# A weight part on a second DMA queue, an image block in two halves, and a later place for the small vectors, at the start of a vision-transformer block

## The reference

```python
# x: 32 images of 3 x 96 x 96; patches of 16 x 16; D = 256, 37 tokens per image (one class token, 36 patches)
patches = patchify(x)                                   # (32, 36, 768)
tokens  = einsum('bnd,ed->bne', patches, W) + b
h       = concatenate([cls_token, tokens], 1) + pos_embedding
paths   = sigmoid(h @ Wp + bp)                          # 8 heads, depth 5
agree   = pq * pk + (1 - pq) * (1 - pk)
sim     = cumprod(agree, -1).sum(-1) / 5                # causal mask, softmax
h       = layernorm(h + softmax(sim) @ (h @ Wv) @ Wo)
y       = silu(layernorm_affine(h) @ w1 + fc1_bias)     # w1, w2 dequantised from int32
h       = layernorm(h + 0.5 * (y @ w2 + fc2_bias))
```

## Time and profile before

| | |
|---|---|
| times of three runs | 176.03, 178.40, 178.91 us |
| profiled execution | 176.34 us |
| span in the trace | 174.6 us |
| PE busy | 154.1 us, 88% of the span |
| DVE, ACT, POOL busy | 94.3, 48.0, 55.6 us |
| first matmul | 6.09 us after the span's start |

### The profile page before, as it was taken

How to read it: one execution, slowest core, us unless ns; L and a number is a source line. 1 busy time by engine, 2 the same in 40 slices (tenths; PEclk the granted TensorE clock), 3 DMA queues, 4 the chain that set the end, 5 groups by cost and what they waited for, 6 DMA issues and landing times.

```text
span 174.6 us, 2987 instructions
## 1 busy us (share of the span) xinstructions
PE 154.1 (88%) x1141; PEld 122.0 (70%) x1141; DVE 94.3 (54%) x175; ACT 48.0 (27%) x105; POOL 55.6 (32%) x129
## 2 busy tenths in 40 slices
PE   0289999799989999899999999999879969979980
PEld 0177878577667797487887778887658858868760
DVE  0065047557777956728647587647547443634232
ACT  0412112523243335114235324226022311032100
POOL 5009811032082603427107218106334022530011
PEclk9999999999999999999999999999999999999999
DMA  5999999700000000000100010000010000000000
GB/s 141 241 241 248 232 369 375 280 2 4 0 2 6 2 0 4 0 0 8 34 0 0 0 34 0 30 4 0 0 32 4 30 0 0 30 34 0 0 30 30
DMA packets 5501, 10.67 MB, mean 61 GB/s; under 512 B 715, under 2 KB 4400, under 8 KB 5232
## 3 DMA queue, kind: packets, MB, share of 16 engines
q1 hardware_dynamic: 5248, 10.30, 20.1%
q10 hardware_dynamic: 240, 0.19, 0.5%
HBM read 9.27 MB, written 1.21 MB: 60 GB/s over the span
## 4 chain that ended last, share of the span: by engine, by line
PE 83%; DVE 6%; DMA 4%; ACT 2%; POOL 2%; issue 1%; ACTq 1%; POOLq 0%
PE bank_z L555 20%; PE bank_s L542 18%; PE bank_z L436 7%; DMA vec_rows<-in_L_ffn_ln_beta 4%; PE bank_s L412 4%; PE bank_p L451 4%; PE bank_s L479 3%; PE bank_p L452 3%; PE bank_s L537 2%; PE bank_w L493 2%; PE bank_p L427 2%; PE bank_o L508 2%; PE bank_o L509 2%; PE bank_z L427 2%; PE bank_o L517 2%; PE bank_w L497 2%
## 5 line engine op out<-in xcount | busy, mean ns | idle before, releaser
L555 PE MATMUL bank_z<-w,act 128*128 128x256 f32 (+1 forms) x160 | 37.0, 381 | 1.8 <-DVE res L830 1.8
L542 PE MATMUL bank_s<-hnT,w 128*128 128x256 f32 (+1 forms) x160 | 35.2, 362 | 0.0
L555 PEld LDWEIGHTS bank_z<-w,act 128*128 128x128 f32 (+1 forms) x160 | 28.1, 182 | 8.0 <-issue 3.2
L542 PEld LDWEIGHTS bank_s<-hnT,w 128*128 128x128 f32 x160 | 28.9, 190 | 5.0
L821 DVE SCALAR_TENSOR_TENSOR act<-th,bank_s 128x512 f32<-128x512 f32 (+1 forms) x20 | 13.0, 648 | 20.3 <-ACT th L691 20.1
L337 POOL TENSOR_TENSOR rstd<-var,exponents 128x3 f32<-128x3 f32 (+1 forms) x10 | 8.9, 893 | 46.9 <-DVE var L805 46.9
L691 ACT ACTIVATE th<-bank_s 128x512 f32<-128x512 f32 (+1 forms) x20 | 11.3, 565 | 32.4 <-PE bank_s L542 32.4
L792 DVE RECIPROCAL recip<-bank_w 128x222 f32<-128x222 f32 (+1 forms) x11 | 16.4, 1494 | 0.7 <-PE bank_w L497 0.7
L675 ACT ACTIVATE phi_q<-bank_p 128x222 f32<-128x222 f32 (+1 forms) x11 | 3.9, 351 | 32.6 <-PE bank_p L461 32.6
L436 PE MATMUL bank_z<-xT,wT 128*128 128x288 f32 x48 | 12.6, 413 | 0.0
L787 DVE TENSOR_TENSOR probs<-probs,allowed 111x888 f32<-111x888 f32 (+1 forms) x11 | 11.5, 1046 | 1.9 <-ACT probs L685 1.9
(11 more groups left out here) (107 smaller groups left out, 242.0 us busy)
## 6 DMA issues: line engine op xcount, KB each, us to landing
x_rows<-in_x SPq DMA_DIRECT2D x6, 576.0 KB, 13.7
q<-in_L_ffn_fc_q SPq DMA_DIRECT2D x2, 1024.0 KB, 20.1
s<-in_L_ffn_fc_scales SPq DMA_DIRECT2D x2, 1024.0 KB, 22.1
out<-fin SPq DMA_DIRECT2D x9, 128.0 KB, 1.7
w_rows<-in_L_tok_W SPq DMA_DIRECT2D x3, 256.0 KB, 8.2
wvp<-in_L_attn_Wv SPq DMA_DIRECT2D x1, 256.0 KB, 10.2
wo<-in_L_attn_Wo SPq DMA_DIRECT2D x1, 256.0 KB, 17.1
b<-in_L_ffn_fc_bias ACTq DMA_DIRECT2D x1, 128.0 KB, 9.6
```

The source lines that it names most:

```text
L542: last = mm(block[:, i], w1[:, e, f * 128:(f + 1) * 128], hnT[p % 2][:, e, 0:n], start=False, stop=(i == 1 and e == E2 - 1))
L555: last = mm(bank_z[0:w, 0:D], act2[:, f, in_pair(b)], w2[:, f, :], start=(f == 0), stop=(f == FB - 1))
```

## The change

Four things change.

The first weight part moves from SP's queue to ACT's, as the first issue there, ahead of `pos_rows` and the vectors. Its size stays.

The first image block is issued first on SP, as two transfers of 8 of the 16 image rows each, with a semaphore for each (`x0_in`). DVE sorts each half as it comes (`by_half_patch`), so `x_pat_ready` counts one more from there on. `turn_block` waits for each half apart.

`turn_vectors` moves on PE from ahead of `turn_block(0)` to between `project_channel(0, 0)` and `project_channel(0, 1)`, and its result from `bank_w` to an unused end of bank 1 of `bank_s` (`vec_bank`). Because of that `turn_block(1)` waits for the last step of `position_columns`.

The order on PE up to the third block is another, and `project_channel` of channel 0 goes by k first and e second.

```diff
@@ SP
-            for c in range(C):
+            top = x[0:HALF, 0].rearrange("b (g o i) w -> b g o (i w)", o=2, i=PATCH // 2)
+            for ih in range(2):
+                sp.dma_start(x_rows[:, 0, ih * HALF_PATCH:(ih + 1) * HALF_PATCH], top[:, :, ih]).then_inc(x0_in[ih], 16)
+            for c in range(1, C):
                 sp.dma_start(w_rows[:, :, c * 256:(c + 1) * 256], w_by_channel[c]).then_inc(w_in[c], 16)
                 x_block(c)
@@ ACT
+            act.dma_start(w_rows[:, :, 0:256], w_by_channel[0]).then_inc(w_in[0], 16)
             act.dma_start(pos_rows[:], pos.rearrange("o t d -> (o t) d")).then_inc(pos_in, 16)
@@ PE
             def turn_block(n):
-                pe.wait_ge(x_pat_ready, n + 1)
                 for ih in range(2):
+                    pe.wait_ge(x_pat_ready, n + 2 if n > 0 else ih + 1)
+                    if n == 1 and ih == 0:
+                        pe.wait_ge(posb_step, 1 + E2)
...
+                order = [(e, k) for e in range(E2) for k in (2 * n, 2 * n + 1)]
+                if n == 0:
+                    order = [(e, k) for k in (0, 1) for e in range(E2)]
...
             turn_weight(0)
-            turn_vectors()
             turn_block(0)
             project_channel(0, 0)
+            turn_vectors()
+            project_channel(0, 1)
             turn_weight(1)
             turn_block(1)
-            pe.wait_ge(posb_step, E2)
-            pe.wait_ge(vec_ready, 1)
-            project_channel(0, 1)
+            project_channel(1, 0)
             turn_weight(2)
-            project_channel(1, 0)
+            project_channel(1, 1)
             turn_block(2)
-            project_channel(1, 1)
             project_channel(2, 0)
@@ DVE
+            def by_half_patch(ih):
+                dve.wait_ge(x0_in[ih], 16)
+                dve.tensor_copy(x_pat[:, 0, :, ih * 128:(ih + 1) * 128].rearrange("p g (i j) -> p g i j", i=PATCH // 2),
+                                x_rows[:, 0, ih * HALF_PATCH:(ih + 1) * HALF_PATCH].rearrange(
+                                    "p (i g j) -> p g i j", i=PATCH // 2, g=GRID)).then_inc(x_pat_ready, 1)
...
-            by_patch(0)
+            by_half_patch(0)
+            by_half_patch(1)
             x_columns(0)
             position_columns()
```

More of the change, by code:

```diff
@@ L46, in vit_block @@
     PARTS = 3
+    HALF_PATCH = PATCH * IMG // 2
     FIRST = NTOK % 128
@@ L108, in vit_block @@
         bank_z = ps("bank_z", [128, 512])
+        vec_bank = bank_s[:, 1, 3 * HR:512]
         ident = sb("ident", [128, 128])
@@ L181, in vit_block @@
         w_in = [sem(f"w_in{i}") for i in range(C)]
+        x0_in = [sem(f"x0_in{i}") for i in range(2)]
         x_in = [sem(f"x_in{i}") for i in range(2 * C)]
@@ L396, in turn_vectors @@
                 pe.wait_ge(weight_set, 5)
+                pe.wait_ge(xT_dve, 1)
                 for e in range(E2):
-                    pe.transpose(bank_w[:, e * T:(e + 1) * T], pos_rows[:, e * 128:(e + 1) * 128], ident[0:T, 0:T])
+                    pe.transpose(vec_bank[:, e * T:(e + 1) * T], pos_rows[:, e * 128:(e + 1) * 128], ident[0:T, 0:T])
                 at = E2 * T
-                pe.transpose(bank_w[:, at:at + N_VEC], vec_rows[:], ident[0:N_VEC, 0:N_VEC])
-                pe.transpose(bank_w[:, at + N_VEC:at + N_VEC + 1], weight_row[:].rearrange("o i a b -> o (i a b)"),
+                pe.transpose(vec_bank[:, at:at + N_VEC], vec_rows[:], ident[0:N_VEC, 0:N_VEC])
+                pe.transpose(vec_bank[:, at + N_VEC:at + N_VEC + 1], weight_row[:].rearrange("o i a b -> o (i a b)"),
                              ident[0:1, 0:1]).then_inc(vec_psum, 1)
             def turn_block(n):
-                pe.wait_ge(x_pat_ready, n + 1)
                 for ih in range(2):
+                    pe.wait_ge(x_pat_ready, n + 2 if n > 0 else ih + 1)
+                    if n == 1 and ih == 0:
+                        pe.wait_ge(posb_step, 1 + E2)
                     if n > 0:
@@ L422, in project_channel @@
                 pe.wait_ge(wT_ready, n + 1)
-                for e in range(E2):
-                    for k in (2 * n, 2 * n + 1):
-                        if c == 0 and e == 0:
-                            pe.wait_ge(xT_act if k % 2 else xT_dve, n + 1)
-                        last = mm(first_half_bank(c, e)[:, 0:CP], wT[:, k, e * 128:(e + 1) * 128], patches(k, c),
-                                  start=(k == 0), stop=(k == KT - 1))
-                    if n == C - 1:
+                order = [(e, k) for e in range(E2) for k in (2 * n, 2 * n + 1)]
+                if n == 0:
+                    order = [(e, k) for k in (0, 1) for e in range(E2)]
+                for e, k in order:
+                    if c == 0 and (k, e) in ((2 * n, 0), (2 * n + 1, 0)):
+                        pe.wait_ge(xT_act if k % 2 else xT_dve, n + 1)
+                    last = mm(first_half_bank(c, e)[:, 0:CP], wT[:, k, e * 128:(e + 1) * 128], patches(k, c),
+                              start=(k == 0), stop=(k == KT - 1))
+                    if k == KT - 1:
                         last.then_inc(tok_psum, 1)
@@ L748, in position_columns @@
                 at = E2 * T
[L749 to L750 removed]
+                dve.tensor_copy(vec_cols[:], vec_bank[:, at:at + N_VEC]).then_inc(posb_step, 1)
+                dve.tensor_copy(weight_col[:], vec_bank[:, at + N_VEC:at + N_VEC + 1]).then_inc(vec_ready, 1)
                 dve.wait_ge(posb_step, 1)
                 for e in range(E2):
[L753 to L754 removed]
+                    ts(posb[:, e, 1:T], vec_bank[:, e * T + 1:(e + 1) * T], tokb_col[:, e:e + 1], None, ALU.add)
+                    tt(posb[:, e, 0:1], vec_bank[:, e * T:e * T + 1], cls_col[:, e:e + 1], ALU.add).then_inc(posb_step, 1)
             def class_tokens():
```

4 lines of the change are left out of this document (removed).

## The result

Twenty executions of the changed kernel had a median of 177.82 us, twenty of the kernel before on the same chips 177.0 us. Every ratio in this document leaves out executions over 1.5% above the fastest of their kernel; the two medians alone would give 1.0046. The ratio is 1.0083 with a 95% interval of 1.0055 to 1.0111: slower by some 1.5 us, where no change was forecast. The base of the forecast, 177.4 us, lay 0.4 us above the median measured for the kernel before, so 177.82 came within 0.4 us of the forecast time although the change itself was missed: that is luck.

The account below looks back on a forecast made before the run. PE bounds the kernel, block 0 its start, with the vectors level. Vectors at 14.0 plus 12.28 us put the third block at 26.28 against 26.25: no change, 177.4 us, between bases 176.4 and 178.4; range 174.2 to 180.8.

Parts of the forecast that it names:

- Landing of block 0's second half (6.5): First loads on SP's queue: second half lands at 6.5 us, no earlier than 6.0 and no later than 8.9.
- The fourth case: Block 0 still lands at 8.4 to 8.9, bound by engines, not queue; 0.0 to +0.5 us; chance 0.12.
- Landing of the vectors (14.0): ACT's queue: vectors land at 14.0 us, bounds 9.6 to 16.6, stalling PE about 2 us from 11.8.
- the second case: Vectors come at 11.8 or before: -2.15 us, 174.2 on the profiled execution, 176.2 on the median; chance 0.18.
- the third case: Vectors land with block 2 at 16.6, PE idle from 11.8: 2.6 to 5.0 us slower, 179.0 to 181.3; chance 0.18.
- Weight part (6.0): First weight part, issued at 0.79 on ACT's queue, lands 5.2 us later, at 6.0.
- Full rate (10.9): PE, working without a break from 6.0, reaches its full rate 4.9 us later, at 10.9.
- The eight rows: Channel 0's four products on block 0, eight matmul rows on PE, run from 9.2 to 11.8, partly at half rate.
- Lost covers (0.4): Projections of channels 1 and 2: second product waits for ACT's copy, 0.2 us each.
- Third block (26.28): PE starts the third block at 14.0 + 12.28 = 26.28 us against 26.25 before: no change.
- Biases on POOL: POOL's first bias step moves from 13.1 to about 18 us, at no cost.

Follow-up runs that it names:

- the split: Changed kernel with the 37 position rows loaded as 32 and 5 rows; ratio 1.0020 to the kernel before.
- loads alone: Kernel before with only the new loads, vectors still turned ahead of block 0; ratio 1.0055 to the kernel before.
- the rows twice: Changed kernel loading the same 37 position rows a second time into a tile nobody reads; ratio 1.0311 to the kernel before.
- before, split: Kernel before with the 37 position rows loaded as 32 and 5 rows; ratio 1.0008 to the kernel before.
- The middle order: Changed kernel with each block again turned ahead of a projection covering its copies, DVE sorting block 1 before its position steps; ratio 1.0020 to the kernel before.

## Why the prediction was wrong

**Landing of block 0's second half (6.5): failed, and it decided when PE came to the vectors.** Measured 9.02, outside the bounds of 6.0 to 8.9 that were given. The value was argued from the queue: nothing stood ahead of it there. But the position rows use one engine, and that engine's six packets of the half start only behind the 37 rows (6.45 to 7.71, the other 90 by 5.74); without the rows beside it the half was early, with the split (6.34) and with the rows issued last (6.45). The prediction knew the one engine and used it against the vectors only. The fourth case (0.12) had the landing nearly right (8.4 to 8.9, and `x_pat` at 9.4, which came at 9.60), though it put it to all engines. The rule of the Trainium skill that was weighed against the change (DMA: Bandwidth & Descriptors, section Issuing engines are not separate DMA queues) is borne out in the time: with the rows split the weight part's queue made no difference (0.9885 and 0.9881). The 9.02 against 8.86 is no test of it, since the rows kept back both.

**Landing of the vectors (14.0): failed.** With these loads they were there at 10.2 (loads alone), and there was no stall; the second case had that (0.18). The sum let the rows wait until the weight part was through at 6.0. It was through at 4.0: issued ahead of the rows it was not kept back by them, and it went side by side with SP's loads (69.5% of the engines). That rows on one engine can come very late was right as a mechanism: PE got them at 17.2 with the rows twice and at 17.1 with the rows last, and 1.031 and 1.047 in the time, which is the third case's stall from another cause.

**Weight part (6.0): mis-sized,** 4.07. The 5.2 us were carried over from before, where the rows kept the part back (with the rows split it came at 3.98 there). The 2 us gave PE nothing, since the next thing was the half.

**Full rate (10.9): failed.** The sum took the 4.9 us from first work to full rate in the trace of before as a rule. It came at 13.4 after, and from 1.8 us after the first product (before, split) to 8.6 us (after, split). The eight rows took 3.22 us and not 2.6. Extra transposes in the idle time left it where it was in two kernels, and in one brought it to 7.1 for a while; what sets the moment stays open.

**Lost covers (0.4): mis-sized,** 1.2, and this is what made the third block late. The chain of the kernel before has, for comparison:

```profile
18.97 0.44 PE bank_s L389 x4
19.41 0.97 PE bank_p L427 x4
20.38 0.97 PE bank_o L427 x4
21.35 0.99 PE bank_s L412 x12
```

Channel 1's first projection takes 2.47 us (18.58 to 21.05) against 0.97 + 0.97 = 1.94 there, 0.5 more; from the turning of block 2 to the third block it is 3.61 us (23.43 to 27.04) against 0.99 + 1.94 = 2.93, 0.7 more. The prediction counted ACT's copy less one product, 0.2 each time. But ahead of channel 2 PE waits 0.45 us for DVE's copy, which had no cover at all and was not in the sum, and the product behind each wait takes longer too (0.75 instead of 0.48, and 1.21 for two instead of 0.97). With the second projection of channel 0 done and block 1 turned, the changed kernel was 0.4 us ahead (18.58 against 18.97 for the same work); 1.2 less 0.4 is the 0.79 of the third block. The middle order, which keeps the covers, has 0.6% less.

**Third block (26.28): the error of 0.8 us** is small by luck. PE came to the vectors at 14.09, where the sum had 14.0, but by another path: not by their landing, which was over at 10.2, but by the late half and the late rate. From there it took 12.95 us and not 12.28: the covers cost 0.8 more than forecast, the rest 0.1 less. Biases on POOL: 14.19 and not 18, harmless either way, as forecast. By its own words (the middle of case 3 between both bases) the upper end of the range would be 181.2 and not 180.8; nothing hangs on it.

**What stays open.** The profile explains 0.79 us of the 1.5. The rest lies in executions that have no trace. The moment of the full rate moves by microseconds from trace to trace here (11.8 to 20.66 in the table); whether it also does so between executions of one kernel, and so makes the rest, is not shown.

## What to carry to other kernels

The load of 37 rows went through one engine, and a large load that used all engines was complete only when that one was done: look for small, early loads of odd sizes before moving the large ones, and split them. When loads are moved, name for each the last engine to finish it, not the queue. And when instructions are moved so that a late input fits in, count what they had covered: here that cost three times what it was thought to.

## What the runs showed of the hardware

Two loads of 256 KB and more on two queues ran side by side at 69.5% and 46.4% of the 16 engines in 0.55 us, and the one on the second queue landed in 3.1 us; on the first queue, with the position rows split, it came as early (PE at 3.89 and 3.98, against 4.07). On the single engine of the 37 rows the last six of a half block's 96 packets started from 6.45 on, behind the rows, when the other 90 had started by 5.74. On the single engine of the 37 rows, doubling the rows moved what stood behind them by 7 us and the large load beside them by nothing. Extra transposes from 1.67 us on did not bring the full rate earlier in two kernels (13.3 against 13.4 and 16.4 against 16.8) and may have in a third (13.5 against 15.2); in the fourth it was there at 7.1 us, still there at 9.2 after 1.22 us without work, and lost from then until 12.7. The column of the granted clock reads 1.00 in the first microseconds of every trace here, while the durations are those of the lower level.
